# A scan beside attention and four experts on one core: idle TensorE products behind the steps of the scan, and another order of work

## The reference

```
h  = layernorm(x)
px = h @ W_state.T + b_state ;  g = sigmoid(h @ W_gate.T + b_gate)
state_t = tanh(px_t + state_{t-1})        # 1024 steps, one after the other
x1 = x + layernorm(g * state)
y  = layernorm(x1) ; hh = rms(y) * n1_w
q, k = rms per head (16 heads of 16), v ; causal softmax(q k / 4) @ v, @ wo.T, channels 0..63 set to 0
y  = y + attention ; xf = rms(y) * n2_w
top-2 of 4 experts by softmax(xf @ gate_w.T); all four experts are computed for all rows:
  e0: gelu(up) -> down          e1: silu(w1) * w2 -> down
  e2: gelu(gelu(gelu(l1) l2) l3) -> l4     e3: gelu(gelu(down) up) -> out
out = x1 + layernorm(y + moe),  moe channels 0..63 set to 0
```

## Time and profile before

| | |
|---|---|
| median of three runs | 1593.18 us |
| the profiled execution's own time | 1590.76 us |
| its span, first to last instruction | 1589.0 us |
| busy PE, DVE, ACT, POOL | 1393.2, 1096.9, 951.8, 317.6 us |
| mean granted TensorE clock | 0.928 of 2.4 GHz |
| MATMULs | 12320 |
| scan, first addition to last tanh | 24.2 to 872.2 us |

### The profile page before, as it was taken

The page is one execution under the profiler, slowest core; times in us unless marked ns, Lnnn a source line. Parts: engine busy times, 40 slices in busy tenths (PEclk is TensorE's granted clock), DMA queues, the critical chain, the costliest instruction groups (busy, mean ns, idle before and its releaser), DMA issues.

```text
span 1589.0 us, 33614 instructions
## 1 busy us (share of the span) xinstructions
PE 1393.2 (88%) x12320; PEld 1104.4 (70%) x12320; DVE 1096.9 (69%) x2884; ACT 951.8 (60%) x2090; POOL 317.6 (20%) x1146
## 2 busy tenths in 40 slices
PE   6905779999976799999999999999999899998997
PEld 3404668889863467778886577866787467875797
DVE  7867486655577967777888766787788667864242
ACT  2535465676555687777565846458544684567931
POOL 3343232223333323322332100001000100000000
PEclk9956579999985889999998999999999999999998
DMA  5584136855654445736666555574756556665443
GB/s 167 147 287 128 35 98 189 259 170 153 197 185 147 130 144 153 222 120 214 203 196 200 163 172 167 187 235 147 226 185 188 180 160 211 188 196 190 126 131 112
DMA packets 235572, 274.35 MB, mean 173 GB/s; under 512 B 36624, under 2 KB 158992, under 8 KB 235152
## 3 DMA queue, kind: packets, MB, share of 16 engines
q1 hardware_dynamic: 235408, 272.19, 56.2%
HBM read 229.98 MB, written 43.45 MB: 172 GB/s over the span
## 4 chain that ended last, share of the span: by engine, by line
PE 64%; DVE 10%; ACT 9%; DMA 7%; issue 4%; POOL 2%; SPq 2%; ACTq 0%; DVEq 0%; POOLq 0%
PE PS L1054 60%; ACT work L1008 3%; PE PS L1057 3%; DMA KT<-ktd 3%; POOL AD L1729 2%; ACT PX L940 2%; PE PS L1138 2%; SPq L862 1%; DVE mx L1528 1%; ACT work L1033 1%; DMA UU<-in_L_attn_x 1%; DMA work<-in_L_ffn_e_l 1%; DVE st L1340 1%; DMA ktd<-KTs 1%; DMA WB<-wlo_e_l 1%
## 5 line engine op out<-in xcount | busy, mean ns | idle before, releaser
L1729 POOL TENSOR_TENSOR AD<-PX 128x8 f32<-128x8 f32 x1023 | 247.7, 242 | 564.7 <-ACT PX L940 548.6
L940 ACT ACTIVATE PX<-AD 128x8 f32<-128x8 f32 x1023 | 219.3, 214 | 230.2 <-POOL AD L1729 227.6
L1008 ACT ACTIVATE work<-PS 128x1024 f32<-128x1024 f32 (+1 forms) x312 | 288.9, 960 | 85.9 <-PE PS L1054 84.7
L1528 DVE TENSOR_REDUCE mx<-PS 128x2 f32<-128x1024 f32 (+3 forms) x224 | 252.3, 1143 | 84.7 <-PE PS L1054 84.3
L1054 PE MATMUL PS<-work,vlx 128*32 128x256 f32 (+2 forms) x2816 | 240.8, 385 | 21.4 <-ACT work L1008 8.5
L1054 PE MATMUL PS<-EP,u_e_l 128*128 128x256 f32 x1024 | 193.7, 284 | 1.6 <-DVE EP L1388 1.4
L1736 POOL TENSOR_SCALAR_AFFINE_SELECT work<-work 128x512 f32<-128x512 f32 x96 | 65.0, 687 | 628.2 <-ACT work L1008 628.2
L1054 PE MATMUL PS<-WB,work 128*128 128x192 f32 x1024 | 182.6, 333 | 4.2 <-ACT work L1033 2.9
L1033 ACT ACTIVATE work<-PS 128x512 f32<-128x512 f32 x176 | 104.4, 597 | 127.6 <-PE PS L1054 125.9
L1054 PE MATMUL PS<-EP,WB 128*128 128x256 f32 x640 | 180.0, 281 | 0.0
L1054 PEld LDWEIGHTS PS<-WB,work 128*128 128x128 f32 x1024 | 167.5, 192 | 10.6 <-issue 6.2
(11 more groups left out here) (175 smaller groups left out, 2345.0 us busy)
## 6 DMA issues: line engine op xcount, KB each, us to landing
KT<-ktd SPq DMA_DIRECT2D x112, 512.0 KB, 4.7
WB<-wlo_e_l SPq DMA_DIRECT2D x160, 256.0 KB, 3.0
WB<-wlo_e_up SPq DMA_DIRECT2D x64, 256.0 KB, 3.1
WB<-wlo_e_w SPq DMA_DIRECT2D x64, 256.0 KB, 3.0
ktd<-KTs SPq DMA_DIRECT2D x112, 128.0 KB, 2.6
WB<-wdn_e_down SPq DMA_DIRECT2D x64, 192.0 KB, 2.5
KT<-ktd SPq DMA_DIRECT2D x48, 256.0 KB, 4.1
KT<-ktd SPq DMA_DIRECT2D x32, 384.0 KB, 4.2
```

Of the source, the lines that this page charges most:

```text
L940: eng.activation(cur, AD[n % 2], ACT.Tanh).then_inc(of(*key), 1)
L1008: eng.activation(pt[:, :, :, q0:L], two("sc", *a).rearrange("p a (l q) -> p a l q", l=2)[:, :, :, q0:L], ACT.Exp).then_inc(of(*key), 1)
L1528: eng.tensor_reduce(o, x, AX, ALU.max, negate=True).then_inc(of(*key), 1)
L1729: eng.tensor_tensor(AD[n % 2], PX[c % 2][:, :, :, t], PX[(n - 1) // L % 2][:, :, :, (n - 1) % L], ALU.add).then_inc(of(*key), 1)
```

## The change

A new function `stay_awake` goes over PE's finished order. Where the planner has a gap between two PE items, it looks for scan steps whose tanh ends in that gap, between 76 and 880 us of planned time. Behind each such step it places a group of one to six products, as many as the planner's 0.107 us each fill of the time to the next step or item less 0.2 us. It leaves a step out where real PE work fills over 0.8 of the 3.4 us around it, or where no PSUM bank is open. An open bank is one whose last owner's readers are all done by then. On the chip a group waits for those readers, for the constants and for its scan step, and then issues `identb` times `maskk` into the bank; nobody reads the result and no semaphore is raised.

The planner no longer doubles PE's durations (`LOW` from 0.38 to 0.0). The tables `START` and `AT` and the prices `STAY` have other numbers, and with them the order of every engine and the buffers. Durations of items, their instructions, and their dependencies stay as they are.

```diff
+AWAKE, SPIN, SPAN, ENOUGH = (76.0, 880.0), 0.107, 3.4, 0.8
-WINDOW, LOW, HIGH, FRESH = 3.413, 0.38, 0.75, 80.0
+WINDOW, LOW, HIGH, FRESH = 3.413, 0.0, 0.75, 80.0
-STAY = {"pe": 24.2, "act": 5.7}
+STAY = {"pe": 23.5, "act": 26.6}
-START = (101.2, 162.6, 177.3, 239.6, 336.5, 416.5, 521.4, 595.3, 735.9, 806.3, 936.0, 1005.2, 1113.3, 1190.3, 1307.3, 1390.6)
+START = (123.1, 123.4, 142.9, 249.7, 336.1, 426.0, 530.7, 579.2, 718.2, 813.2, 942.9, 1018.5, 1115.1, 1203.2, 1292.6, 1373.5)
-AT = {"piece": (-133.2, 84.2, 12.4, 109.4),
+AT = {"piece": (-241.2, 93.5, -139.7, 128.5),
...
+def stay_awake(P):
+    pe = P.order["pe"]
+    streams = [(P.start[k], P.start[k] + P.items[k][1]) for k in pe]
+    over = lambda k: P.start[k] + P.took[k] + P.items[k][5] + HOP
...
+    seen = [(over(("stanh", n)), n) for n in range(1, T)] + [(1e6, T)]
+    order, at = [], 0
+    for i, k in enumerate(pe):
+        e0, s1 = (P.start[pe[i - 1]] + P.took[pe[i - 1]] if i else 0.0), P.start[k]
+        while seen[at][0] < max(e0 - 0.3, AWAKE[0]):
+            at += 1
+        while seen[at][0] < min(s1 - 0.35, AWAKE[1]):
+            t, n = seen[at]
+            at += 1
+            room = min(seen[at][0], s1) - max(t, e0) - 0.2
+            near = sum(max(0.0, min(b, t + 0.6 * SPAN) - max(a, t - 0.4 * SPAN)) for a, b in streams)
+            count = min(6, int(room / SPIN))
+            bank = open_bank(max(t, e0))
+            if near > ENOUGH * SPAN or count < 1 or bank is None:
+                continue
+            key = ("spin", n, count)
...
+            order.append(key)
+        order.append(k)
+    P.order["pe"] = order
+    return P
-    return P.run()
+    return stay_awake(P.run())
+                if kind == "spin":
+                    n, count = a
+                    for x in freed(key, "P0"):
+                        pe.wait_ge(*x)
+                    pe.wait_ge(*done("consts"))
+                    pe.wait_ge(*done("stanh", n))
+                    for i in range(count):
+                        mm(PS[:, place[key, "P0"], 0:256], identb, maskk.rearrange("p l q -> p (l q)"), True, True)
+                    continue
```

More of the change, by code:

```diff
@@ new lines @@
+STAY = {"pe": 23.5, "act": 26.6}
+START = (123.1, 123.4, 142.9, 249.7, 336.1, 426.0, 530.7, 579.2, 718.2, 813.2, 942.9, 1018.5, 1115.1, 1203.2, 1292.6, 1373.5)
+AT = {"piece": (-241.2, 93.5, -139.7, 128.5),
+      "post": (21.2, 99.6, -30.1, -13.0),
+      "prep": (12.9, -79.6, -55.3, -12.4),
+      "value": (-129.4, 123.2, -79.8, -118.8),
+      "key": (-21.3, -56.4, 45.6, 36.4),
+      "query": (-78.3, 7.8, -106.3, -70.8),
+      "max": (-150.5, -115.0, -61.1, -54.7),
+      "maxima": (59.3, 8.2, -48.1, 56.6),
+      "bound": (-78.4, 6.7, 62.2, 93.0),
+      "score": (-31.9, 100.0, 16.9, 40.7),
+      "scores": (19.8, 10.7, 19.1, 17.1),
+      "av": (59.1, -19.8, 10.1, 13.3),
+      "merge": (23.4, -47.5, -7.8, 8.1),
+      "out": (-315.1, -160.8, -279.2, -72.0),
+      "gate": (-143.5, -83.5, -267.5, -121.3),
+      "l1": (11.9, 239.7, 280.4, 272.0),
+      "e0up": (123.0, 139.7, -41.7, 394.5),
+      "l2": (261.2, 330.9, 180.0, 286.0),
+      "e0dn": (314.4, 336.2, 355.6, -132.8),
+      "e1": (286.9, 303.1, 305.9, 163.9),
+      "l3": (213.3, 310.8, 255.5, 177.2),
+      "e3dn": (242.3, 367.7, 224.3, 261.9),
+      "e1dn": (480.5, 313.2, 288.2, 386.1),
+      "l4": (228.4, 235.0, 149.6, 415.6),
+      "e3up": (431.0, 320.8, 254.0, 395.6),
+      "e3out": (211.0, 323.4, 363.1, 423.0),
+      "fin": (265.2, 175.8, 203.8, 375.6)}
@@ L211, in run, with open_bank @@
         return self
+def stay_awake(P):
+    pe = P.order["pe"]
+    streams = [(P.start[k], P.start[k] + P.items[k][1]) for k in pe]
+    over = lambda k: P.start[k] + P.took[k] + P.items[k][5] + HOP
+    takes = defaultdict(list)
+    for (k, p), i in P.place.items():
+        for j in range(i, i + BANKS.get(p, 0)):
+            takes[j].append((P.start[k], P.items[k][3][p]))
+    for j in takes:
+        takes[j].sort(key=lambda x: x[0])
+    def open_bank(t):
+        best = None
+        for j in takes:
+            before = [x for x in takes[j] if x[0] < t]
+            last = max((over(x) for x in before[-1][1]), default=0.0) if before else 0.0
+            if last < t and (best is None or last < best[0]):
+                best = (last, j, before[-1][1] if before else ())
+        return best
+    seen = [(over(("stanh", n)), n) for n in range(1, T)] + [(1e6, T)]
[14 more added lines that the diff above has]
+            key = ("spin", n, count)
+            P.items[key] = ("pe", count * SPIN, 0.0, {}, "128", 0.0)
+            P.feeds["stanh", n].append(key)
+            P.start[key], P.took[key] = max(t, e0), count * SPIN
+            P.place[key, "P0"], P.turn[key, "P0"] = bank[1], bank[2]
+            streams.append((max(t, e0), max(t, e0) + count * SPIN))
+            order.append(key)
+        order.append(k)
+    P.order["pe"] = order
+    return P
 def tiles_of_time(u):
```

## The result

Slower. Four runs took 1611.86 to 1623.45 us, median 1616.73; four runs of the kernel before have the median 1593.29. The ratio of the means is 1.0159, 95% interval 1.0114 to 1.0205 (that of the medians is 1.0147). The forecast was 1569, faster, in 1535 to 1605. The clock did nearly what I had forecast and the time did the opposite. Two of the six executions of the third kernel of experiment 1 (1627.08 and 1627.22 us) count as slow and are left out of its ratio; all other executions in this document are fast ones.

What follows compares the result with a forecast made beforehand. PE was taken as the bound, except in two low-clock holes (80 to 257 and 457 to 604 us). From 1590.76 us: -20 clock, +6 products, -8 order gave 1568.8, said as 1569; range 1535 to 1605.

Steps and rivals of the forecast that it cites:

- The clock: PE between 80 and 880 us: idle products restore full clock, 20 us faster, ends 0 and 40.4.
- the first hole: 80 to 257 us, where PE's clock is low; forecast to rise to 0.93 or more, as in 457 to 604 us.
- the 20.6 us ahead of 257 us: PE time saved for units 0 to 3 in 80 to 257 us; nearly all arrives at unit 3's end, 7 us counted.
- my ceiling of 40.4 us: Most that full clock could take out of PE's busy time in the low-clock stretches: 20.6, 16.1 and 3.7 us.
- The products: Idle products in PE's gaps delay ready work behind them: 6 us slower, ends 0 and 25.
- Rival 3: Groups tie PE to a late scan, mainly in 457 to 604 us: slower, 1609 us; chance 0.15.
- The order: New order on all engines: 8 us gained, a tenth of reachable PE idle time; bounds 25 gained, 30 lost.
- Table loads: ACT's two groups of 57 and 49 loads, 106 in all; a higher price of changing mode brings them under 85.
- The transposes: If transposes get no full clock, as the skill says, 4 us less gain in 457 to 604 us: 1573.
- the third that I took: Share of a busy PE microsecond at the lower clock that full clock returns, taken between 28% and 41%.

Runs made afterwards that it cites:

- the third kernel of experiment 1: The changed kernel with its groups' wait for the scan step taken out; ratio 1.0133 to the kernel before.
- the thin ones: Groups with products 16 columns wide instead of 256, waits kept; ratio to the kernel before 1.0016 on the old order, 1.0303 on the new.
- groups and fills: Kernel before (old order) with 172 groups, plus products in idle gaps over 0.65 us that its trace shows without a group; ratio 0.9887.
- filled twice: Either order with groups and products in traced idle gaps over 0.65 us, then in those left over 0.4 us; to kernel before: old 0.9919, new 0.9984.
- filled once: Either order with groups, plus products in traced idle gaps over 0.65 us without a group; ratio to kernel before: old 0.9887, new 1.0045.

## Why the prediction was wrong

**The clock.** The step held for the clock itself (0.93 or more was forecast for the first hole, 0.97 came; for the second 0.91). Its worth depends on the order. On the new order the groups give 1.4 points, 22 us, where I had 20 for the clock less 6 for the products; unit 3's last down product ends at 461.5 us without them and at 444.4 with them. So this term did not make the miss. On the old order, from whose rows I had worked it out, it did not hold. I said that nearly all of the 20.6 us ahead of 257 us would arrive at unit 3's end, as PE is at its bound from 257 us on. Unit 3's feed-forward part ends at 459 us with the groups (in an execution of 1603.3 us) and at 454 before (1590.8 us). PE's share of those 177 us grew by products, not by work. Half of my ceiling of 40.4 us (20) was the term; groups on the old order gave 2 to 5 us (0.15% in all, 0.3% against the thin ones), groups and fills 18. My reading, argued and not tested, is that units 0 and 1 go at the pace of the scan, DVE and transfers, and that only what is saved where PE bounds arrives.

**The products.** 6 us, measured 2 to 3 (0.16% with thin ones on the old order). Rival 3 had the sign and not the cause: groups tied to the scan made PE wait 13.5 us, and without these waits the ratio did not change beyond its interval.

**The order.** This is the step that failed. I took a gain of 8 us from bounds of -25 and +30, by the share of idle time that an order can reach. Measured +3.0%, some 47 us, outside my bounds; 22 us of it come back by the groups, and 25 are left. A likely cause stood before me in the diff: `LOW` at 0.0 makes the planner count on full clock always. I read it as freedom for a better order. It also means that every stretch in which the chip grants less is later than the plan, on PE, then on ACT, which stands in its own list before PE's results, and so on the scan. No run changed `LOW` or one of the tables alone, so that it was `LOW` is not shown. The new order alone has a mean clock of 0.92 in 257 to 419 us, where the old one has 1.00, and 0.73 against 0.76 in 457 to 604:

```profile
257.00:419.00 162.00, 149.49 (x1427) 136.84 (x1427) 82.79 (x225) 93.74 (x263) 41.17 (x173) 0.92 0.61 178
457.00:604.00 147.00, 97.04 (x759) 67.08 (x761) 107.33 (x285) 79.85 (x240) 47.77 (x179) 0.73 0.44 130
```

Of the 3.0 points 1.4 to 2.3 go as both orders come near full clock. My bounds came from PE's idle time and left out that PE's busy time depends on the order as well, through the clock. Table loads, of which I expected under 85 in the two groups, rose from 106 to 114; a higher price of a change of mode did not mean fewer of them.

```profile
L1083 ACT ACT_TABLE_LOAD x61 | 78.3, 1283 | 48.0 <-PE PS L1104 47.4
L1058 ACT ACT_TABLE_LOAD x53 | 68.0, 1283 | 32.4 <-PE PS L1104 31.8
```

**The transposes.** The 4 us that I weighed for transposes without the full clock decided nothing here.

**What stays open.** The 0.65 (filled twice) to 1.6 points (filled once) between the orders at nearly equal clock. The planner has the new order 11 us ahead; the chip has it 10 us behind when both are filled twice. Of the 24 us by which the changed kernel's span is longer than before, 12 are idle time of PE behind 880 us (56 against 44), at clock 0.98 in both; filled once, the new order has 39 us there and the old 33. The lag of the new order filled still grows between unit 4's maxima and its last scores, by 6 us, with the clock at 1.00. Which of the moved items it is, I did not try.

## What to carry to other kernels

Idle products pay most in the gaps that the trace shows, not in those that the plan has: on the old order 308 products in 33 measured gaps gave 1.0 point (0.9985 to 0.9887, intervals apart), and 620 products in 172 planned ones 0.15 to 0.3. When a cost model is relaxed together with the trick that is to make the relaxation true, run the new schedule without the trick and the trick on the old schedule first; the two numbers here (1.030 and 0.9985) would have settled it. A low mean clock does not say what a stretch has to give: groups took 80 to 201 us of the old order from 0.59 to 0.89, and unit 1's maxima came no earlier.

## What the runs showed of the hardware

In the changed kernel gaps of 1.97 and 2.28 us were followed by 10 and 20 us at the lower clock, though PE was then busy nearly all of the time (10.00 of 10.00 us, 19.91 of 20.30, half of the latter with groups). Ahead of the first PE had been busy 9.29 of 9.30 us. Not every such gap costs the clock: behind one of 1.81 us (ahead of 270.6 us) and one of 2.33 us (ahead of 113.9 us) it stayed at 1.00. By the third that I took for a busy microsecond at the lower clock, an estimate, the two stretches cost 3.3 and 6.6 us of PE's time. Thirteen unneeded products in 1.59 us cost nothing where PE would have waited. Eight scores took 1.13 us behind the empty gap and 0.67 us behind the filled one.
